# An FFN block product taken out of its accumulation chain and given one full PSUM bank

## The chip, the cores and the metric

The kernel runs on one core of a Trainium2 chip. The time is the device time of one execution in microseconds (us); the median of three runs stands below, and one further execution was profiled. The core's engines run side by side and meet through semaphores: TensorE (PE: matmuls into PSUM; PEld is its weight load), VectorE (DVE), ScalarE (ACT), GpSimd (POOL) and SyncE (SP), which here only issues DMA transfers.

## The reference

Each of the 64 samples of x (64 x 1024) is mixed across its 64 channels with one of 16 condition matrices, then passed through a 1024 x 1024 matrix with a top-1 routed rank-8 correction, and added to x:

```
W = weights[condition];   y = einsum('bct,bcd->bdt', x, W)
logits = y_flat @ gate_w.T + expert_bias;   one_hot = one_hot(argmax(logits))
base   = einsum('bth,oh->bto', y, W_up)
z      = einsum('nh,erh->ner', y_flat, lora_A);   d = einsum('ner,ehr->neh', z, lora_B)
out    = x + base + einsum('neh,ne->nh', d, one_hot)
```

## The kernel before

The 64 samples are taken four at a time, so there are 16 blocks of 256 rows (two tiles t of 128 rows). A block's y and W_up are cut into 2 x 2 parts, and the product is made with seven half-size products (Strassen's scheme with shared sums) in place of eight: `a11`, `a12`, `a22`, `s1`, `s2`, `s4`, `s3`, in the text also p1 (`a11`), p2 (`a12`), p6 (`s2`), p5 (`s1`), p7 (`s3`), p4 (`a22`). Each operand is split into a high and a low part (fp32r), and a product of 512 output columns is 4 (k) x 3 (part pairs) steps; a step is one matmul of 512 columns, or two matmuls into two neighbouring PSUM banks. The two-bank form exists because four of the products also carry 36 router and LoRA columns (292 + 256 columns).

PSUM: `bank_x` and `bank_y` are pairs of banks, `bank_b` and `bank_c` single banks, `y_ps` a pair for the conditioned y. In block q one pair is the "chain" and holds running sums: p1, then p1+p6 (U2), then p1+p6+p7 (U3), then U3+p4 plus the second LoRA correction, which is c21. The other is the "pair": p2 and the first LoRA correction (c11's rest), and a transpose of the second z. Chain and pair change roles from block to block (`chains[par]`, `chains[1 - par]`). c11, c12, c21, c22 are the four quarters of the block's output; DVE adds each PSUM result into the x rows in SBUF (`add_pair` reads 2 x 256 columns of two banks, `add_bank` 512 columns of one), and SP stores them.

The order on every engine is written out by hand in `period(q, par, closing)`; nothing is reordered by a scheduler. Block 0 is written out in the start-up, blocks 1 to 14 run in a loop of two periods a turn, and block 15 is the closing period. In period q, PE makes block q's products, and between them `make_y` for block q+1, four times (t, half): (0,0) after p6, (0,1) after the first LoRA correction, (1,0) after p7, (1,1) after `s4` and its correction. Each `make_y` waits for `y_summed`: the DVE addition `sum_y` that empties `y_ps` of the one before. `make_y` (1,1) so waits for `sum_y(a21, ...)`. The y chain goes on: `make_y` -> ACT `move_small_y` -> DVE `sum_y` -> for the last part POOL `add_s1`, `add_s2` -> ACT `round_s1`, `round_s2` -> DVE `low_operand` -> PE `s1`, `s2`. In DVE's period, `after_p7` and `route(q, 1)` stand directly ahead of `sum_y(a21, ...)`.

Of the kernel before, what the change touches and what calls it, by code (L numbers as in the profile page):

```python
# [5 lines left out]
def adaln_ffn_kernel(  # L6
# [8 lines left out]
    lora_b: bass.AP,  # L15
    out: bass.AP,
):

# [16 lines left out]
    ALU = mybir.AluOpType  # L37
# [7 lines left out]
    P = 128  # L45
# [6 lines left out]
    GC = E + ER  # L52
    BANK = 512
    QUARTER = BANK // 2
    BLOCKS = B // 4
# [13 lines left out]
    with ctx:  # L69
# [6 lines left out]
        def sem(name):  # L76
            return ctx.enter_context(nc.semaphore(name))
# [48 lines left out]
        bank_b = banks("bank_b", 1)  # L126
        bank_c = banks("bank_c", 1)
        y_ps = banks("y_ps", 2)
        chains = [bank_x, bank_y]

        ident_zero = sem("ident_zero")
        ident_done = sem("ident_done")
# [32 lines left out]
        p1_out = sem("p1_out")  # L165
        u2_out = sem("u2_out")
        u3_out = sem("u3_out")
        p5_out = sem("p5_out")
        route_step = sem("route_step")
        z_turned = sem("z_turned")  # L170
# [188 lines left out]
        def _(act):  # L359
# [68 lines left out]
            def move_z(q, par, t, used):  # L428
                act.wait_ge(z_turned, 2 * q + t + 1)
                if used:  # L430
                    act.wait_ge(delta22 if t else delta12, q)
                src = chains[1 - par][:, 1, 0:P] if t else bank_c[:, 0, 0:P]
                act.activation(z_t[t][:, :], src, ACT.Copy).then_inc(z_ready, 1)

            split_x(0, 0, 0, False)
# [84 lines left out]
        def _(pe):  # L520
# [63 lines left out]
            def multiply(op, q, bank, fresh):  # L584
                pe.wait_ge(low[op], q + 1)
                w = w_of[op]
                if op in ROUTED:
                    pieces = [(bank[:, 0, 0:QUARTER + GC], slice(0, QUARTER + GC)),
                              (bank[:, 1, 0:QUARTER], slice(QUARTER + GC, WIDE))]
                elif op == "a22":  # L590
                    pieces = [(bank[:, 0, 0:QUARTER], slice(0, QUARTER)),
                              (bank[:, 1, 0:QUARTER], slice(QUARTER, BANK))]
                else:
                    pieces = [(bank[:, 0, :], slice(0, BANK))]
                for k in range(KH):
                    for a, b in ((0, 0), (0, 1), (1, 0)):
                        for dst, cols in pieces:
                            mm = pe.matmul(dst, hl[op][:, a, k, :], w[:, b, k, cols],  # L598
                                           start=(fresh and k == 0 and a + b == 0),
                                           stop=(k == KH - 1 and a == 1), skip_group_check=not fresh)  # L600
                mm.then_inc(product_done[op], 1)
# [4 lines left out]
            def add_delta_pair(t, bank):  # L606
                for n in range(2):
                    mm = add_delta(t, bank[:, n, 0:QUARTER], lora_b_hl[:, n * QUARTER:(n + 1) * QUARTER])
                return mm
# [9 lines left out]
            def delta12_of(q):  # L619
                add_delta(0, bank_c[:, 0, :], lora_b_hl[:, BANK:O]).then_inc(delta12, 1)  # L620

            def last_product(q, chain):
                pe.wait_ge(u3_out, q + 1)
                multiply("a22", q, chain, False)

            def second_delta(q, chain):
                pe.wait_ge(z_ready, 2 * q + 2)
                add_delta_pair(1, chain).then_inc(delta21, 1)
                pe.wait_ge(p5_out, q + 1)
                add_delta(1, bank_b[:, 0, :], lora_b_hl[:, BANK:O]).then_inc(delta22, 1)  # L630

# [63 lines left out]
            make_y(1, 0, 1, index[0])  # L695
            pe.wait_ge(turned_low, AT["lora", 1] + 1)
            turn_z(bank_c[:, 0, 0:P], 0, 0)
            last_product(0, bank_x)
            delta11_of(0, bank_y)
            make_y(1, 1, 0, index[1])  # L700
            multiply("s4", 0, bank_c, True)
            delta12_of(0)
            turn_second_z(0, bank_y)
            make_y(1, 1, 1, index[1])
            second_delta(0, bank_x)

            def period(q, par, closing):
                chain, pair = chains[par], chains[1 - par]
                pe.wait_ge(c11_out, q)
                multiply("a11", q, chain, True)  # L710
                index = [None, None]
                if not closing:
                    index[0] = load_index(q + 1, 0)
                pe.wait_ge(c21_out, q)
                multiply("a12", q, pair, True)
                pe.wait_ge(p1_out, q + 1)
                multiply("s2", q, chain, False)
                if not closing:
                    make_y(q + 1, 0, 0, index[0])
                pe.wait_ge(c12_out, q)  # L720
                turn_z(bank_c[:, 0, 0:P], q, 0)
                pe.wait_ge(c22_out, q)
                multiply("s1", q, bank_b, True)
                delta11_of(q, pair)
                if not closing:
                    make_y(q + 1, 0, 1, index[0])
                pe.wait_ge(u2_out, q + 1)
                multiply("s3", q, chain, False)
                if not closing:
                    index[1] = load_index(q + 1, 1)  # L730
                    make_y(q + 1, 1, 0, index[1])
                multiply("s4", q, bank_c, True)
                delta12_of(q)
                if not closing:
                    make_y(q + 1, 1, 1, index[1])
                turn_second_z(q, pair)
                last_product(q, chain)
                second_delta(q, chain)

            in_blocks(pe, period)  # L740

# [1 line left out]
        def _(dve):  # L743
# [39 lines left out]
            def score(bank, addend):  # L783
                dve.tensor_tensor(scores[:, :], bank[:, 0, QUARTER:QUARTER + GC], addend[:, :], ALU.add)\
                   .then_inc(route_step, 1)
# [24 lines left out]
            def add_pair(bank, par, t, half):  # L810
                return dve.tensor_tensor(wide(x_part(par, t, half)), bank[:, :, 0:QUARTER], wide(x_part(par, t, half)),  # L811
                                         ALU.add)
# [3 lines left out]

            def after_p1(q, par):
                dve.wait_ge(product_done["a11"], q + 1)
                dve.tensor_tensor(partial[:, :], chains[par][:, 0, QUARTER:QUARTER + GC], bias_sb[:, :], ALU.add)
                add_pair(chains[par], par, 0, 0).then_inc(p1_out, 1)  # L820

            def after_p2(q, par, used=True):
                dve.wait_ge(product_done["a12"], q + 1)
                dve.wait_ge(p1_out, q + 1)
                score(chains[1 - par], partial)
                route(q, 0, used)

            def after_p6(q, par):
                dve.wait_ge(product_done["s2"], q + 1)
                add_pair(chains[par], par, 0, 1).then_inc(u2_out, 1)  # L830

            def after_p5(q, par):
                dve.wait_ge(product_done["s1"], q + 1)
# [2 lines left out]

            def after_delta11(q, par):
                dve.wait_ge(delta11, q + 1)
                add_pair(chains[1 - par], par, 0, 0).then_inc(c11_out, 1)

            def after_p7(q, par):
                dve.wait_ge(product_done["s3"], q + 1)
                score(chains[par], bias_sb)
                add_pair(chains[par], par, 1, 1).then_inc(u3_out, 1)

            def after_delta12(q, par):
                dve.wait_ge(delta12, q + 1)
# [2 lines left out]

            def after_delta21(q, par):
                dve.wait_ge(delta21, q + 1)
                add_pair(chains[par], par, 1, 0).then_inc(c21_out, 1)

            def after_delta22(q, par):
                dve.wait_ge(delta22, q + 1)
# [70 lines left out]
            after_delta12(0, 0)  # L927
            low_operand("a12", a12, 1)
            sum_y(a22, 1, 1, 1)

            def period(q, par, closing):
                after_delta21(q - 1, 1 - par)
                low_operand("s1", s1_sum, q)
                low_operand("s2", s2_sum, q)
                after_delta22(q - 1, 1 - par)
                after_p1(q, par)
                if not closing:
                    for b in range(2):
                        split_x(q + 1, 1 - par, 0, b)
                after_p2(q, par)  # L940
                low_operand("s4", a12, q)
                low_operand("s3", a21, q)
                after_p6(q, par)
                low_operand("a22", a22, q)
                if not closing:
                    split_x(q + 1, 1 - par, 1, 0)
                    sum_y(a11, q + 1, 0, 0)
                    split_x(q + 1, 1 - par, 1, 1)
                    low_operand("a11", a11, q + 1)
                after_p5(q, par)  # L950
                after_delta11(q, par)
                if not closing:
                    sum_y(a12, q + 1, 0, 1)
                    low_operand("a12", a12, q + 1)
                after_p7(q, par)
                route(q, 1)
                if not closing:
                    sum_y(a21, q + 1, 1, 0)
                after_delta12(q, par)
                if not closing:  # L960
                    sum_y(a22, q + 1, 1, 1)

            in_blocks(dve, period)
            after_delta21(BLOCKS - 1, (BLOCKS - 1) % 2)
            after_delta22(BLOCKS - 1, (BLOCKS - 1) % 2)


# [21 lines left out]
```

## Time and profile before

| | |
|---|---|
| median of 3 runs | 445.52 us (444.39 to 446.64) |
| the profiled execution, its own time | 445.25 us |
| its span, first to last instruction | 443.4 us |
| PE busy | 433.8 us, 98% |
| PE weight loads busy | 411.3 us, 93% |
| DVE busy | 351.4 us, 79% |
| ACT busy | 198.3 us, 45% |
| POOL busy | 116.7 us, 26% |
| DMA | 87 GB/s over the span |

Busy shares are averages over the span. PE instructions overlap in the pipeline, so that the duration of a matmul is longer than the distance from its start to the next one's; costs of a group are read as distances between starts. The same holds for DVE, to a lesser degree.

### The profile page before, as it was taken

Reading aid. Unit: us, or ns where it says so; the run is one execution under the profiler, and the core shown is the slowest. Engines: PE = TensorE matmul, PEld = TensorE weight load, DVE = VectorE, ACT = ScalarE, POOL = GpSimd, SP = SyncE. Lnnn points to the kernel's source line nnn. Section 1 sums busy time; section 2 is a strip of 40 time slices with the busy share of each in tenths; the row PEclk is TensorE's granted clock in tenths of the full one; section 3 lists DMA queues with packets and bytes.
Section 4 is the critical chain, followed back from the end, with each engine's and each line's share of the span. In section 5 each row is a group of like instructions: output and inputs, shape, how many; then the busy total and the mean of one; then the engine's idle time right before and its main releaser. Section 6 shows DMA issues by size and latency. Waiting matters only on the chain.

```text
span 443.4 us, 8927 instructions
## 1 busy us (share of the span) xinstructions
PE 433.8 (98%) x3138; PEld 411.3 (93%) x3139; DVE 351.4 (79%) x643; ACT 198.3 (45%) x310; POOL 116.7 (26%) x95
## 2 busy tenths in 40 slices
PE   8899998999999999999999999999999999999996
PEld 8789997999999999999999999999999999999995
DVE  3899879698796969789686969879696978969653
ACT  4895436253544426244543625354352624454210
POOL 3992040130505022050504013050503204050400
PEclk9999999999999999999999999999999999999999
DMA  9900032130412122140313113041212214032102
GB/s 216 406 21 1 2 120 71 54 139 24 148 41 104 61 89 100 47 142 24 118 56 109 71 51 138 24 139 50 98 67 94 95 47 142 24 118 70 50 30 90
DMA packets 17231, 38.73 MB, mean 87 GB/s; under 512 B 3838, under 2 KB 3838, under 8 KB 17218
## 3 DMA queue, kind: packets, MB, share of 16 engines
q1 hardware_dynamic: 16018, 38.02, 24.3%
q10 hardware_dynamic: 1040, 0.26, 0.3%
q0 software_dynamic: 160, 0.28, 0.3%
q8 instruction: 8, 0.13, 0.1%
q14 instruction: 5, 0.04, 0.0%
HBM read 21.78 MB, written 16.78 MB: 87 GB/s over the span
## 4 chain that ended last, share of the span: by engine, by line
PE 82%; DVE 6%; issue 6%; POOL 2%; DMA 2%; ACT 0%; DVEq 0%; POOLq 0%
PE bank_y L598 25%; PE bank_x L598 24%; PE y_ps L534 11%; PE bank_c L598 10%; PE bank_b L598 9%; DMA lora_b_sb<-in_L_ffn_lora_B_dram 2%; DVE w_s L780 1%; DVE w_a L780 1%; DVE x_hl L747 1%; PE bank_y L604 1%; PE bank_c L604 1%; PE bank_x L604 1%; PE bank_b L604 1%; POOL lora_b L305 1%; DVE hl_s L757 1%
## 5 line engine op out<-in xcount | busy, mean ns | idle before, releaser
L310 POOL TENSOR_TENSOR s_sum<-a 128x512 f32<-128x512 f32 x16 | 20.7, 1293 | 294.7 <-DVE a L752 294.7
L368 ACT ACTIVATE x_hl<-x_sb 64x1024 fp32r<-64x1024 f32 x64 | 67.8, 1059 | 58.9 <-DMA x_sb<-in_x_dram 58.1
L747 DVE TENSOR_TENSOR x_hl<-x_sb,x_hl 64x1024 fp32r<-64x1024 f32 x64 | 78.2, 1221 | 9.1 <-ACT x_hl L368 7.2
L598 PE MATMUL bank_x<-w_a,hl_a 128*128 128x292 f32 (+1 forms) x576 | 76.1, 288 | 0.0
L598 PE MATMUL bank_y<-w_a,hl_a 128*128 128x292 f32 (+1 forms) x576 | 76.0, 288 | 0.0
L598 PEld LDWEIGHTS bank_y<-w_a,hl_a 128*128 128x128 f32 x576 | 73.6, 189 | 0.5
L598 PEld LDWEIGHTS bank_x<-w_a,hl_a 128*128 128x128 f32 x576 | 73.5, 189 | 0.5
L372 ACT ACTIVATE y_small<-y_ps 128x512 f32<-128x512 f32 x62 | 37.1, 599 | 74.1 <-PE y_ps L534 74.1
L534 PE MATMUL y_ps<-cond_hl,x_hl 128*128 x496 | 63.8, 272 | 2.5 <-DVE a L752 1.0
L534 PEld LDWEIGHTS y_ps<-cond_hl,x_hl 128*128 128x128 f32 x496 | 61.5, 191 | 5.0 <-DVE a L752 1.4
L752 DVE TENSOR_TENSOR a<-y_ps,y_small 128x512 f32<-128x512 f32 x62 | 42.6, 686 | 13.0 <-ACT y_small L372 12.4
L598 PE MATMUL bank_y<-w_s,hl_s 128*128 128x292 f32 (+1 forms) x384 | 51.5, 290 | 1.2 <-DVE x_sb L811 1.2
L598 PE MATMUL bank_x<-w_s,hl_s 128*128 128x292 f32 (+1 forms) x384 | 51.5, 290 | 0.0
L598 PEld LDWEIGHTS bank_y<-w_s,hl_s 128*128 128x128 f32 x384 | 49.2, 188 | 1.4 <-DVE x_sb L811 1.4
L598 PEld LDWEIGHTS bank_x<-w_s,hl_s 128*128 128x128 f32 x384 | 49.4, 188 | 0.1
L598 PE MATMUL bank_b<-w_s,hl_s 128*128 128x512 f32 x192 | 48.3, 400 | 0.0
L598 PE MATMUL bank_c<-w_s,hl_s 128*128 128x512 f32 x192 | 48.2, 399 | 0.0
L378 ACT ACTIVATE hl_a<-a 128x512 fp32r<-128x512 f32 x48 | 30.1, 627 | 40.2 <-DVE a L752 40.2
L757 DVE TENSOR_TENSOR hl_a<-a,hl_a 128x512 fp32r<-128x512 f32 x48 | 33.6, 700 | 10.6 <-ACT hl_a L378 10.2
L598 PEld LDWEIGHTS bank_c<-w_s,hl_s 128*128 128x128 f32 x192 | 35.0, 189 | 7.3
L598 PEld LDWEIGHTS bank_b<-w_s,hl_s 128*128 128x128 f32 x192 | 35.2, 190 | 6.8
L811 DVE TENSOR_TENSOR x_sb<-bank_y,x_sb 128x512 f32<-128x512 f32 x40 | 27.3, 682 | 16.2 <-PE bank_y L604 16.0
(126 smaller groups left out, 476.5 us busy)
## 6 DMA issues: line engine op xcount, KB each, us to landing
x_sb<-in_x_dram SPq DMA_DIRECT2D x32, 512.0 KB, 3.4
out_dram<-x_sb SPq DMA_DIRECT2D x64, 256.0 KB, 2.0
w_raw<-in_L_ffn_W_up_dram SPq DMA_DIRECT2D x8, 512.0 KB, 11.7
cond_sb<-in_L_cond_weights_dram ACTq DMA_DIRECT2D x1, 256.0 KB, 5.5
cond_sb<-in_L_cond_weights_dram SPq DMA_DIRECT2D x1, 256.0 KB, 6.6
router_sb<-in_L_ffn_lora_A_dram POOLq DMA_DIRECT2D x1, 128.0 KB, 8.1
lora_b_sb<-in_L_ffn_lora_B_dram POOLq DMA_DIRECT2D x1, 128.0 KB, 8.4
router_sb<-in_L_ffn_gate_w_dram POOLq DMA_DIRECT2D x1, 16.0 KB, 6.1
```

Source lines behind the costliest of these rows:

```text
L310: pool.tensor_tensor(s1_sum[:, :], a21[:, :], a22[:, :], ALU.add).then_inc(s1_added, 1)
L368: act.activation(x_hl[rows, t, b, :], x_sb[rows, 2 * par + t, :], ACT.Copy).then_inc(x_high, 1)
L372: act.activation(to[:, :].rearrange("q (g d) -> q g d", d=D), halves_of(bank)[:, :, 1, :], ACT.Copy).then_inc(y_small_out, 1)
L378: act.activation(hl[op][:, 0, :, :], src[:, :].rearrange("q (k n) -> q k n", n=P), ACT.Copy)\
L534: mm = pe.matmul(bank[:, k % KH // 2, at:at + P], x_hl[:, t, b, k * P:(k + 1) * P], cond_hl[:, index[b], :, :], start=True, stop=True)
L598: mm = pe.matmul(dst, hl[op][:, a, k, :], w[:, b, k, cols], start=(fresh and k == 0 and a + b == 0), stop=(k == KH - 1 and a == 1), skip_g ...
L604: return pe.matmul(dst, z_t[t][:, :], src, start=False, stop=True, skip_group_check=True)
L747: dve.tensor_tensor(x_hl[other, t, b, :], x_sb[rows, 2 * par + t, :], x_hl[rows, t, b, :].bitcast(fp32), ALU.subtract).then_inc(x_low, 1)
L752: dve.tensor_tensor(dst[:, :].rearrange("q (g d) -> q g d", d=D), halves_of(bank)[:, :, 0, :], small[:, :].rearrange("q (g d) -> q g d", d ...
L757: dve.tensor_tensor(hl[op][:, 1, :, :], src[:, :].rearrange("q (k n) -> q k n", n=P), hl[op][:, 0, :, :].bitcast(fp32), ALU.subtract).then ...
L780: dve.tensor_tensor(turn_target(op, c, 1), bank.rearrange("q (k n) -> q k n", n=P), turn_target(op, c, 0).bitcast(fp32), ALU.subtract).the ...
L811: return dve.tensor_tensor(wide(x_part(par, t, half)), bank[:, :, 0:QUARTER], wide(x_part(par, t, half)), ALU.add)
```

## The change

From block 1 on the roles are fixed: the chain is always in `bank_y` and the pair always in `bank_x` (block 0 keeps its own). p4 isn't added to the chain any more: it starts fresh in the first bank of the pair, as 12 matmuls of 512 columns, once p2's bank has been read; its LoRA correction is one matmul of 512 columns. DVE adds U3 from the chain into the x rows by an instruction of its own (`add_u3`), behind `route(q, 1)`, and later adds p4 with its correction by `add_bank`. The semaphore `chain_free` tells PE that the chain's banks may be overwritten, and orders the two additions. On DVE, `after_delta21`, the low parts of s1 and s2 and `after_delta22` move from the head of period q+1 to the tail of period q, which in the instruction stream is the same place.

```diff
-        chains = [bank_x, bank_y]
+        def chain_of(q):
+            return bank_x if isinstance(q, int) and q == 0 else bank_y
+
+        def pair_of(q):
+            return bank_y if isinstance(q, int) and q == 0 else bank_x
...
+        chain_free = sem("chain_free")
...
-                elif op == "a22":
+                elif op == "a22" and not fresh:
                     pieces = [(bank[:, 0, 0:QUARTER], slice(0, QUARTER)),
                               (bank[:, 1, 0:QUARTER], slice(QUARTER, BANK))]
...
             def period(q, par, closing):
-                chain, pair = chains[par], chains[1 - par]
+                chain, pair = chain_of(q), pair_of(q)
                 pe.wait_ge(c11_out, q)
+                pe.wait_ge(chain_free, q)
                 multiply("a11", q, chain, True)
...
                 turn_second_z(q, pair)
-                last_product(q, chain)
-                second_delta(q, chain)
+                multiply("a22", q, pair, True)
+                pe.wait_ge(z_ready, 2 * q + 2)
+                add_delta(1, pair[:, 0, :], lora_b_hl[:, 0:BANK]).then_inc(delta21, 1)
+                delta22_of(q)
...
+            def add_u3(q, par):
+                add_pair(chain_of(q), par, 1, 0).then_inc(chain_free, 1)
...
             def after_delta21(q, par):
                 dve.wait_ge(delta21, q + 1)
-                add_pair(chains[par], par, 1, 0).then_inc(c21_out, 1)
+                if isinstance(q, int) and q == 0:
+                    add_pair(bank_x, par, 1, 0).then_inc(c21_out, 1)
+                else:
+                    dve.wait_ge(chain_free, q + 1)
+                    add_bank(bank_x, par, 1, 0).then_inc(c21_out, 1)
...
                 after_p7(q, par)
                 route(q, 1)
+                add_u3(q, par)
                 if not closing:
                     sum_y(a21, q + 1, 1, 0)
```

On DVE, the stretch from the last steps of `route(q, 1)` to the c22 addition, in a loop period that has its chain in `bank_y`. Before, with `a<-y_ps,y_small` being `sum_y`, first a21 and then a22:

```order
131 L792 REGISTER_ALU
132 L807 TENSOR_TENSOR z_parts<-z_sel,z_parts 128x2x32 [waits route_step]
133 L752 TENSOR_TENSOR a<-y_ps,y_small 128x512 [waits y_small_out]
134 L815 TENSOR_TENSOR x_sb<-bank_c,x_sb 128x512 [waits p5_out,delta12]
135 L752 TENSOR_TENSOR a<-y_ps,y_small 128x512 [waits y_small_out]
136 L811 TENSOR_TENSOR x_sb<-bank_y,x_sb 128x512 [waits delta21]
137 L757 TENSOR_TENSOR hl_s<-s_sum,hl_s 128x512 [waits high_s1]
138 L757 TENSOR_TENSOR hl_s<-s_sum,hl_s 128x512 [waits high_s2]
139 L815 TENSOR_TENSOR x_sb<-bank_b,x_sb 128x512 [waits u3_out,delta22]
```

The same stretch in the changed kernel:

```order
130 L799 REGISTER_ALU
131 L814 TENSOR_TENSOR z_parts<-z_sel,z_parts 128x2x32 [waits route_step]
132 L818 TENSOR_TENSOR x_sb<-bank_y,x_sb 128x512
133 L759 TENSOR_TENSOR a<-y_ps,y_small 128x512 [waits y_small_out]
134 L822 TENSOR_TENSOR x_sb<-bank_c,x_sb 128x512 [waits p5_out,delta12]
135 L759 TENSOR_TENSOR a<-y_ps,y_small 128x512 [waits y_small_out]
136 L822 TENSOR_TENSOR x_sb<-bank_x,x_sb 128x512 [waits chain_free,delta21]
137 L764 TENSOR_TENSOR hl_s<-s_sum,hl_s 128x512 [waits high_s1]
138 L764 TENSOR_TENSOR hl_s<-s_sum,hl_s 128x512 [waits high_s2]
```

One instruction, `add_u3` (132), has come between the routing steps and `sum_y` of a21; the c21 addition reads one bank where it read two, and waits for `chain_free` too.

On PE, from p4 to the next block's p1, before:

```order
356 L598 MATMUL bank_y<-w_a,hl_a 128x256 [waits low_a22,u3_out]
357 L598 MATMUL bank_y<-w_a,hl_a 128x256 x23
358 L604 MATMUL bank_y<-lora_b_hl,z_t 128x256 [waits z_ready]
359 L604 MATMUL bank_y<-lora_b_hl,z_t 128x256
360 L604 MATMUL bank_b<-lora_b_hl,z_t 128x512 [waits p5_out]
361 L585 REGISTER_ALU [waits c11_out]
362 L598 MATMUL bank_x<-w_a,hl_a 128x292 [waits low_a11]
```

The same place in the changed kernel:

```order
356 L605 MATMUL bank_x<-w_a,hl_a 128x512 [waits low_a22]
357 L605 MATMUL bank_x<-w_a,hl_a 128x512 x11
358 L611 MATMUL bank_x<-lora_b_hl,z_t 128x512 [waits z_ready]
359 L611 MATMUL bank_b<-lora_b_hl,z_t 128x512 [waits p5_out]
360 L592 REGISTER_ALU [waits chain_free,c11_out]
361 L605 MATMUL bank_y<-w_a,hl_a 128x292 [waits low_a11]
```

24 matmuls of 256 columns have become 12 of 512, two correction matmuls one, the wait for `u3_out` is gone, and p1 of the next block waits for `chain_free` beside `c11_out`.

## Rows read from the trace of the kernel before

**Rows 1.** The page, part 1: busy time (share of the span) and instructions

```profile
PE 433.8 (98%) x3138; PEld 411.3 (93%) x3139; DVE 351.4 (79%) x643; ACT 198.3 (45%) x310; POOL 116.7 (26%) x95
```

**Rows 2.** The page, part 4: chain that ended last, by engine

```profile
PE 82%; DVE 6%; issue 6%; POOL 2%; DMA 2%; ACT 0%; DVEq 0%; POOLq 0%
```

**Rows 3.** Timeline of PE, start us, duration us, second half of period 7

```profile
228.23 0.40 PE L604 MATMUL bank_x<-lora_b_hl,z_t 128*128 128x256 f32 x2
228.47 1.04 PE L534 MATMUL y_ps<-cond_hl,x_hl 128*128 x8
229.34 3.25 PE L598 MATMUL bank_y<-w_s,hl_s 128*128 128x292 f32 x24
...
233.31 3.01 PE L598 MATMUL bank_c<-w_s,hl_s 128*128 128x512 f32 x12
236.16 0.40 PE L604 MATMUL bank_c<-lora_b_hl,z_t 128*128 128x512 f32 x1
236.40 1.00 PE L534 MATMUL y_ps<-cond_hl,x_hl 128*128 x8
237.24 0.30 PE L613 MATMUL bank_x<-ident,z_parts 128*128 128x128 f32 x1
237.29 3.12 PE L598 MATMUL bank_y<-w_a,hl_a 128*128 128x256 f32 x24
240.25 0.40 PE L604 MATMUL bank_y<-lora_b_hl,z_t 128*128 128x256 f32 x2
240.48 0.39 PE L604 MATMUL bank_b<-lora_b_hl,z_t 128*128 128x512 f32 x1
```

**Rows 4.** Timeline of DVE, period 7; in brackets idle before, and releaser

```profile
230.84 0.68 DVE L811 TENSOR_TENSOR x_sb<-bank_x,x_sb 128x512 f32<-128x512 f32 x1
231.43 0.68 DVE L752 TENSOR_TENSOR a<-y_ps,y_small 128x512 f32<-128x512 f32 x1
232.81 0.69 DVE L757 TENSOR_TENSOR hl_a<-a,hl_a 128x512 fp32r<-128x512 f32 x1 [0.70 <-ACT hl_a L378]
...
235.42 0.68 DVE L752 TENSOR_TENSOR a<-y_ps,y_small 128x512 f32<-128x512 f32 x1
...
238.07 0.69 DVE L752 TENSOR_TENSOR a<-y_ps,y_small 128x512 f32<-128x512 f32 x1 [0.78 <-ACT y_small L372]
240.69 0.69 DVE L811 TENSOR_TENSOR x_sb<-bank_y,x_sb 128x512 f32<-128x512 f32 x1 [1.93 <-PE bank_y L604]
...
242.22 1.55 DVE L757 TENSOR_TENSOR hl_s<-s_sum,hl_s 128x512 fp32r<-128x512 f32 x1 [0.15 <-ACT hl_s L378]
```

**Rows 5.** Timeline of PE, `make_y` of periods 1, 6 and 14, part (1,1)

```profile
84.17 1.00 PE L534 MATMUL y_ps<-cond_hl,x_hl 128*128 x8
...
211.05 1.01 PE L534 MATMUL y_ps<-cond_hl,x_hl 128*128 x8
...
413.55 1.00 PE L534 MATMUL y_ps<-cond_hl,x_hl 128*128 x8
```

**Rows 6.** Timeline of DVE, `sum_y` of a21 in periods 1 and 14

```profile
83.19 0.68 DVE L752 TENSOR_TENSOR a<-y_ps,y_small 128x512 f32<-128x512 f32 x1
...
412.54 0.68 DVE L752 TENSOR_TENSOR a<-y_ps,y_small 128x512 f32<-128x512 f32 x1
```

**Rows 7.** Timeline of PE, period 2, where `make_y` (0,1) came late

```profile
101.31 0.39 PE L604 MATMUL bank_y<-lora_b_hl,z_t 128*128 128x256 f32 x2
101.65 1.11 PE L534 MATMUL y_ps<-cond_hl,x_hl 128*128 x8
102.59 0.60 PE L598 MATMUL bank_x<-w_s,hl_s 128*128 128x292 f32 x3
```

**Rows 8.** Timeline of DVE, period 2, `sum_y` of a11 ahead of it

```profile
100.90 0.69 DVE L752 TENSOR_TENSOR a<-y_ps,y_small 128x512 f32<-128x512 f32 x1 [0.27 <-ACT y_small L372]
```

**Rows 9.** Timeline of ACT, period 7: the x rows' split, and `round_s2`

```profile
224.69 2.14 ACT L368 ACTIVATE x_hl<-x_sb 64x1024 fp32r<-64x1024 f32 x2 [3.15 <-DMA x_sb<-in_x_dram]
...
241.55 0.63 ACT L378 ACTIVATE hl_s<-s_sum 128x512 fp32r<-128x512 f32 x1 [0.75 <-POOL s_sum L314]
```

More of the change, by code:

```diff
@@ L431, in move_z @@
                     act.wait_ge(delta22 if t else delta12, q)
-                src = chains[1 - par][:, 1, 0:P] if t else bank_c[:, 0, 0:P]
+                src = pair_of(q)[:, 1, 0:P] if t else bank_c[:, 0, 0:P]
                 act.activation(z_t[t][:, :], src, ACT.Copy).then_inc(z_ready, 1)
@@ L620, in delta12_of, with delta22_of @@
                 add_delta(0, bank_c[:, 0, :], lora_b_hl[:, BANK:O]).then_inc(delta12, 1)
[L622 to L628, printed above, removed]
+            def delta22_of(q):
                 pe.wait_ge(p5_out, q + 1)
@@ L697, in _ @@
             turn_z(bank_c[:, 0, 0:P], 0, 0)
-            last_product(0, bank_x)
+            pe.wait_ge(u3_out, 1)
+            multiply("a22", 0, bank_x, False)
             delta11_of(0, bank_y)
@@ L704, in _ @@
             make_y(1, 1, 1, index[1])
-            second_delta(0, bank_x)
+            pe.wait_ge(z_ready, 2)
+            add_delta_pair(1, bank_x).then_inc(delta21, 1)
+            delta22_of(0)
             def period(q, par, closing):
-                chain, pair = chains[par], chains[1 - par]
+                chain, pair = chain_of(q), pair_of(q)
                 pe.wait_ge(c11_out, q)
+                pe.wait_ge(chain_free, q)
                 multiply("a11", q, chain, True)
@@ L818, in after_p1 @@
                 dve.wait_ge(product_done["a11"], q + 1)
-                dve.tensor_tensor(partial[:, :], chains[par][:, 0, QUARTER:QUARTER + GC], bias_sb[:, :], ALU.add)
-                add_pair(chains[par], par, 0, 0).then_inc(p1_out, 1)
+                part = dve.tensor_tensor(partial[:, :], chain_of(q)[:, 0, QUARTER:QUARTER + GC], bias_sb[:, :], ALU.add)
+                if isinstance(q, int) and q == 0:
+                    part.then_inc(chain_free, 1)
+                add_pair(chain_of(q), par, 0, 0).then_inc(p1_out, 1)
             def after_p2(q, par, used=True):
@@ L824, in after_p2 @@
                 dve.wait_ge(p1_out, q + 1)
-                score(chains[1 - par], partial)
+                score(pair_of(q), partial)
                 route(q, 0, used)
@@ L829, in after_p6 @@
                 dve.wait_ge(product_done["s2"], q + 1)
-                add_pair(chains[par], par, 0, 1).then_inc(u2_out, 1)
+                add_pair(chain_of(q), par, 0, 1).then_inc(u2_out, 1)
             def after_p5(q, par):
@@ L838, in after_delta11 @@
                 dve.wait_ge(delta11, q + 1)
-                add_pair(chains[1 - par], par, 0, 0).then_inc(c11_out, 1)
+                add_pair(pair_of(q), par, 0, 0).then_inc(c11_out, 1)
             def after_p7(q, par):
                 dve.wait_ge(product_done["s3"], q + 1)
-                score(chains[par], bias_sb)
-                add_pair(chains[par], par, 1, 1).then_inc(u3_out, 1)
+                score(chain_of(q), bias_sb)
+                add_pair(chain_of(q), par, 1, 1).then_inc(u3_out, 1)
+            def add_u3(q, par):
+                add_pair(chain_of(q), par, 1, 0).then_inc(chain_free, 1)
             def after_delta12(q, par):
@@ L852, in after_delta21 @@
                 dve.wait_ge(delta21, q + 1)
-                add_pair(chains[par], par, 1, 0).then_inc(c21_out, 1)
+                if isinstance(q, int) and q == 0:
+                    add_pair(bank_x, par, 1, 0).then_inc(c21_out, 1)
+                else:
+                    dve.wait_ge(chain_free, q + 1)
+                    add_bank(bank_x, par, 1, 0).then_inc(c21_out, 1)
             def after_delta22(q, par):
@@ L929, in _ @@
             sum_y(a22, 1, 1, 1)
+            after_delta21(0, 0)
+            low_operand("s1", s1_sum, 1)
+            low_operand("s2", s2_sum, 1)
+            after_delta22(0, 0)
             def period(q, par, closing):
[L932 to L935, printed above, removed]
                 after_p1(q, par)
@@ L961, in period @@
                     sum_y(a22, q + 1, 1, 1)
+                after_delta21(q, par)
+                if not closing:
+                    low_operand("s1", s1_sum, q + 1)
+                    low_operand("s2", s2_sum, q + 1)
+                after_delta22(q, par)
             in_blocks(dve, period)
-            after_delta21(BLOCKS - 1, (BLOCKS - 1) % 2)
-            after_delta22(BLOCKS - 1, (BLOCKS - 1) % 2)
 _INS = ['x', 'itok_B_0_15', 'L0_cond_weights', 'L0_ffn_W_up', 'L0_ffn_gate_w', 'L0_ffn_expert_bias',
```

## The prediction

> **What bounds the kernel now.** I read the page first. PE is busy for 98% of the span and its weight loads for 93% [rows 1], and the chain that ended last lies on PE for 82% [rows 2]; what isn't PE in it lies nearly all in the start-up. So from block 1 on the kernel is a PE stream, and the naive reading is: what shortens a product shortens the kernel, and DVE, at 79%, has room for one more addition. Whether it has that room where the addition is put decides this case, so I went on to the timelines of one loop period, PE and DVE beside each other. The reader is to see three things there.
>
> First, PE's period. `make_y` (1,1) starts at 84.17 in period 1 and at 413.55 in period 14: 13 periods in 329.38 us, 25.34 us each [rows 5].
>
> Second, how tight DVE is behind PE. DVE ends `sum_y` of a21 at 235.42 + 0.68 = 236.10, and PE starts the `make_y` that needs it at 236.40 [rows 3, 4]. In periods 1 and 14 the same distance is 84.17 - 83.87 = 0.30 and 413.55 - 413.22 = 0.33 [rows 5, 6]; over all 14 it is 0.30 to 0.35. DVE's 21% of idle time isn't at this place. It is in front of other instructions: 0.70 us for ACT's rounding of a12, 0.78 for ACT's copy of the small y, 1.93 for the second LoRA correction [rows 4].
>
> Third, what PE pays when `sum_y` is late. Period 2 has such a case at `make_y` (0,1): the addition, itself 0.27 us late through ACT, ended at 100.90 + 0.69 = 101.59 [rows 8], PE began `make_y` 0.06 us later at 101.65, and from the start of the correction ahead to the start of the next product it took 102.59 - 101.31 = 1.28 us [rows 7], where period 7 took 229.34 - 228.23 = 1.11 [rows 3], and the periods with an early addition 1.08. Over the blocks this distance reads 1.00 us plus the time from the correction's start to the addition's end, never under 1.08. For PE a wait costs from the point at which the addition ends 0.08 us behind the correction's start, because the weights of the first matmul have to be loaded behind the wait too.
>
> **The change part by part.**
>
> p4's form. Before, 24 matmuls of 256 columns run from 237.29 to 240.25: 2.96 us. The form that it gets is that of `s4`, 12 of 512 columns from 233.31 to 236.16: 2.85 us [rows 3]. Saving 0.11 us per block. The correction pair takes 240.48 - 240.25 = 0.23, a single one of 512 columns 236.40 - 236.16 = 0.24 [rows 3]: nothing. 15 blocks are changed, so PE's own work shrinks by 15 x 0.11 = 1.6 us. The Trainium skill ("TensorE: Matmul & The Clock Gate", "Back-to-back issue gap") has N/2.4 + 2.5 ns a matmul, by which 12 matmuls fewer give back only 12 x 2.5 = 30 ns a product, 0.45 us in all; the rows say 110 ns, and the sum goes by the rows.
>
> The wait for `u3_out` before p4. U3's addition follows p7 and is over long before 237.29, and PE shows no gap there [rows 3]: removing it gives 0. The new wait for `chain_free` before p1 sits at 240.7; the flag is set by an addition that ends near 236.1 on DVE: 0, with 4.6 us of cover. p2 still waits for c21, as before, and the reads of the fixed pair keep their distances to their writers: 0.
>
> The c21 addition reads 512 columns of one bank in place of 2 x 256; both forms take 0.68 to 0.69 us: 0.
>
> `add_u3`, once per block, is the new work: a 128x512 addition out of PSUM. Back to back such additions start 231.43 - 230.84 = 0.59 us apart, and take 0.68 alone [rows 4]. It stands in front of `sum_y` of a21, and there DVE works without a pause: from 232.81 to 236.10 no row has an idle time before it. So `sum_y` ends 0.60 us later against the DVE work ahead of it (bounds: 0.59 and 0.69, for an instruction behind the short ones of `route`). The Trainium skill ("VectorE: DVE Perf Modes", "The TRN2 errata") gives 120 + FD cycles of 0.96 GHz for VectorE out of PSUM, 658 ns for 512 columns; by it the sum below would be 14 x 0.06 = 0.8 us higher.
>
> What it costs there. Now the addition ends 236.10 - 236.16 = -0.06 us from the correction's start; with `add_u3` it ends at +0.54. The free point is +0.08, so PE stands for 0.46 us at `make_y` (1,1), in each of the periods 1 to 14. The closing period makes no y and doesn't pay.
>
> Can DVE win this back over the period? Only if the chain from one `make_y` (1,1) to the next has a gap that waits for PE. I followed it: `make_y` -> ACT -> `sum_y` of a22 (238.07) -> POOL, two additions -> ACT `round_s2` (241.55) -> DVE's low part of s2 at 242.22, which waited for just that (0.15) and not for PE [rows 4, 9] -> then DVE without a pause, or the store and load of x that hang on its c22 addition and end at ACT's split at 224.69 [rows 9] -> `sum_y` of a11 -> ... -> the 0.70 us round trip to ACT -> `route` -> `sum_y` of a21. No link is PE's. From 211.05 to 236.10 this chain takes 25.05 us [rows 4, 5]; over the 13 periods the same distance has a mean of 25.02. With 0.60 for `add_u3`, 0.06 until PE starts, and 0.10 for the exposed weight load (`make_y` lasts 1.11 where it waited, 1.00 where it didn't [rows 5, 7]) the loop becomes 25.78 us, against 25.34. The two workings agree: +0.44 and +0.46.
>
> Where p4's saving goes: p4 isn't in that loop. PE comes 0.11 us earlier to `make_y` (0,1) of the next period and waits there 0.11 longer, since it is already at the edge (1.11 against 1.08 in period 7 [rows 3]). It is kept only for the last two blocks, where no such wait follows: -0.2 us.
>
> Sum: 14 x 0.46 - 0.2 = +6.2 us, against the profiled execution's 445.25 (span 443.4). The median of the runs shown is 445.52, 0.3 higher, so that I put the forecast at 451.5, +1.3%.
>
> **The rivals.**
>
> A, the addition is hidden after all, and only PE's saving is left: 15 x -0.11 = -1.6 us, 443.8. For it speaks DVE's idle time, 3.4 us in the rows shown [rows 4], over five times what is added. It decides if the slack at `make_y` (1,1) is over 0.60; the rows show 0.14 (0.08 + 0.06), and all the idle time behind the place of `add_u3`, which cannot help. This is the rival on the other side, and it would lie within 0.5%. Chance 8%.
>
> B, a part is hidden: the loop is less rigid than I read it, as where the DMA of x sometimes ends the chain at ACT rather than DVE (0.27 us idle [rows 8]) or POOL and DVE slow each other less once their work has shifted (the low part of s2 takes 1.55 us beside POOL, others 0.69 [rows 4]). If half of the 0.46 is won back: 14 x 0.23 = +3.2, 448.6. Chance 12%.
>
> C, more is lost: the inserted addition costs its full 0.69 and PE's wait exposes more of the pipeline, 0.55 to 0.65 per period: +7.5 to +9, 453 to 454.5. For it speaks that the instructions of `route` ahead are short, so less may overlap. Chance 12%.
>
> D, the single-bank form and the removed wait give more than the rows show, and the kernel gets faster by over 0.5% (2.2 us, 443.3): it needs rival A and 0.15 us per block. Chance 2%.
>
> **How the numbers follow.** The likeliest case holds 66%, and its own range is 450.5 to 452.7. With B and C the range is 448.4 to 453.6; outside are A, D and the ends of C. A measurement of this kernel tells about 0.5%, 2.2 us, from no change: slower by more takes the likeliest case, C and nearly all of B, 0.88; within 0.5% are most of A and the rest of B, 0.10; faster 0.02.
>
> **What the changed kernel's profile would show.** PE's period of about 25.8 us instead of 25.34; an idle time before `make_y` (1,1) with DVE's `sum_y` as releaser, some 0.3 to 0.5 us in each of 14 periods, and a distance from the correction ahead to the product behind of 1.59 us where it was 1.13 (237.29 - 236.16); p4 in 2.85 us; at `make_y` (0,1) waits of 0.1 to 0.3 us in most periods; PE's busy share down by about 2 points, DVE's busy time up by 15 x 0.68 = 10 us. DVE's idle time before the c21 addition should fall only by p4's 0.11, to 1.8 us, since what comes before it hangs on the same `make_y`. Wrong would make it: a `sum_y` of a21 that ends less than 0.3 us later against the correction than before, or a wait for PE inside the chain that I called free of it.

## The result and the profile after

The changed kernel takes 451.25 us (451.04 to 451.68, 5 runs) where the kernel before, run beside it, takes 445.32 us (444.39 to 446.64): a ratio of 1.0139, 95% interval 1.0128 to 1.0151. By the ratio it is slower by 6.2 us; the two medians are 5.9 us apart, which is inside the interval (5.7 to 6.7). The profiled execution took 451.25 us, its span is 449.4 us.

Of the page after, the busy times and the shares of the chain that ended last (before: [rows 1], [rows 2]):

```profile
PE 437.7 (97%) x2943; PEld 400.8 (89%) x2944; DVE 360.5 (80%) x658; ACT 198.2 (44%) x310; POOL 116.1 (26%) x95
...
issue 50%; DVE 18%; PE 14%; POOL 9%; DMA 5%; ACT 4%; DVEq 0%; POOLq 0%; SPq 0%; ACTq 0%
```

195 matmuls fewer, 9.1 us more of DVE, and a chain of the end that was 82% PE is now 14% PE: it goes through DVE, POOL, ACT and the DMA of x. In every second period it also runs over p4 and the c21 addition behind it; that this piece doesn't set the pace is not read from the chain but shown by experiment 2. The busy share of PE hardly moves, 98% to 97%, although PE no longer sets the pace; the chain says it, the share doesn't.

The list of waits of the kernel after (engine, line, releaser: us in total, times, longest):

```profile
DVE x_sb L822 <- PE bank_x L611: 27.9, 15, 2.4
...
PEld y_ps L541 <- DVE a L759: 10.9, 20, 1.2
```

PE's weight loads for `make_y` wait 10.9 us for `sum_y`, in 20 places. The same line of the kernel before has 1.4 us in 2 places:

```profile
PEld y_ps L534 <- DVE a L752: 1.4, 2, 1.2
```

Timeline of PE in the kernel after: the second half of a loop period, to be laid beside [rows 3], and the `make_y` (1,1) of the first and the last period:

```profile
84.16 1.11 PE L541 MATMUL y_ps<-cond_hl,x_hl 128*128 x8 [0.19 <-DVE a L759]
...
230.25 0.40 PE L611 MATMUL bank_x<-lora_b_hl,z_t 128*128 128x256 f32 x2
230.49 1.10 PE L541 MATMUL y_ps<-cond_hl,x_hl 128*128 x8
231.43 3.24 PE L605 MATMUL bank_y<-w_s,hl_s 128*128 128x292 f32 x24
...
238.25 0.39 PE L611 MATMUL bank_c<-lora_b_hl,z_t 128*128 128x512 f32 x1
238.83 1.11 PE L541 MATMUL y_ps<-cond_hl,x_hl 128*128 x8 [0.20 <-DVE a L759]
239.78 0.30 PE L620 MATMUL bank_x<-ident,z_parts 128*128 128x128 f32 x1
239.83 2.99 PE L605 MATMUL bank_x<-w_a,hl_a 128*128 128x512 f32 x12
242.65 0.40 PE L611 MATMUL bank_x<-lora_b_hl,z_t 128*128 128x512 f32 x1
...
419.61 1.11 PE L541 MATMUL y_ps<-cond_hl,x_hl 128*128 x8 [0.20 <-DVE a L759]
```

Timeline of DVE in the kernel after, the same period, to be laid beside [rows 4]:

```profile
234.89 0.69 DVE L764 TENSOR_TENSOR hl_a<-a,hl_a 128x512 fp32r<-128x512 f32 x1 [0.70 <-ACT hl_a L385]
...
237.35 0.23 DVE L814 TENSOR_TENSOR z_parts<-z_sel,z_parts 128x64 f32<-128x64 f32 x1
237.49 0.68 DVE L818 TENSOR_TENSOR x_sb<-bank_y,x_sb 128x512 f32<-128x512 f32 x1
238.09 0.68 DVE L759 TENSOR_TENSOR a<-y_ps,y_small 128x512 f32<-128x512 f32 x1
238.69 0.68 DVE L822 TENSOR_TENSOR x_sb<-bank_c,x_sb 128x512 f32<-128x512 f32 x1
240.61 0.69 DVE L759 TENSOR_TENSOR a<-y_ps,y_small 128x512 f32<-128x512 f32 x1 [1.24 <-ACT y_small L379]
243.09 0.69 DVE L822 TENSOR_TENSOR x_sb<-bank_x,x_sb 128x512 f32<-128x512 f32 x1 [1.79 <-PE bank_x L611]
```

The reader is to see: `add_u3` at 237.49, `sum_y` of a21 behind it, over at 238.77, and `make_y` (1,1) beginning 0.06 us later at 238.83. Its bracket shows only 0.20 us of idle PE, since the pipelined ends of the matmuls ahead cover the rest. Read it as a distance: from the correction at 238.25 to p4 at 239.83 it is 1.58 us, against 1.13 before. All 14 periods show it (1.55 to 1.59), and (419.61 - 84.16) / 13 gives 25.80 us a period, where [rows 5] gave 25.34. Thirteen periods longer by 0.46 make 6.0 us, which is the difference of the two spans, 449.4 - 443.4. The fourteenth stall is the one ahead of 84.16, and it doesn't show there, because this execution came 0.36 us earlier out of its start-up: the first `make_y` (0,1) starts at 54.45, in the profiled execution of the kernel before at 54.81. p4 takes 242.65 - 239.83 = 2.82 us here and 2.85 in the mean of the periods, where it took 2.96, and hardly anything of that is seen in the time.

### The profile page after: what moved, and what is told of

Its sections match the earlier page's. It is cut to its first block, busy times and chain, and to the rows that moved or that the text cites. A ratio compares the mean times of both kernels' runs of the same rounds, so it can differ in the third digit from the quotient of the medians.

```text
span 449.4 us, 8559 instructions
## 1 busy us (share of the span) xinstructions
PE 437.7 (97%) x2943; PEld 400.8 (89%) x2944; DVE 360.5 (80%) x658; ACT 198.2 (44%) x310; POOL 116.1 (26%) x95
## 4 chain that ended last, share of the span: by engine, by line
issue 50%; DVE 18%; PE 14%; POOL 9%; DMA 5%; ACT 4%; DVEq 0%; POOLq 0%; SPq 0%; ACTq 0%
PE bank_x L605 5%; POOL a L324 3%; DMA x_sb<-in_x_dram 3%; POOL s_sum L321 3%; POOL s_sum L317 3%; DVE x_sb L818 3%; DVE x_sb L822 2%; PE bank_x L639 2%; DVE a L759 2%; PE bank_y L605 2%; DVE x_hl L754 2%; DMA out_dram<-x_sb 2%; PE y_ps L541 2%; DVE hl_a L764 2%; DVE hl_s L764 2%
## 5 line engine op out<-in xcount | busy, mean ns | idle before, releaser
L605 PE MATMUL bank_x<-w_a,hl_a 128*128 128x292 f32 (+2 forms) x588 | 99.4, 323 | 0.0
L605 PE MATMUL bank_y<-w_s,hl_s 128*128 128x292 f32 x720 | 96.6, 290 | 1.2 <-DVE x_sb L818 1.2
L605 PEld LDWEIGHTS bank_y<-w_s,hl_s 128*128 128x128 f32 x720 | 92.3, 188 | 1.4 <-DVE x_sb L818 1.4
L605 PEld LDWEIGHTS bank_x<-w_a,hl_a 128*128 128x128 f32 x588 | 85.2, 189 | 6.7
L541 PEld LDWEIGHTS y_ps<-cond_hl,x_hl 128*128 128x128 f32 x496 | 60.4, 191 | 13.0 <-DVE a L759 10.9
L541 PE MATMUL y_ps<-cond_hl,x_hl 128*128 x496 | 66.1, 276 | 4.9 <-DVE a L759 3.4
L605 PEld LDWEIGHTS bank_y<-w_a,hl_a 128*128 128x128 f32 x384 | 50.5, 188 | 1.5
L605 PE MATMUL bank_y<-w_a,hl_a 128*128 128x292 f32 (+1 forms) x384 | 51.1, 288 | 0.0
L818 DVE TENSOR_TENSOR x_sb<-bank_y,x_sb 128x512 f32<-128x512 f32 x61 | 41.5, 680 | 0.2 <-PE bank_y L605 0.2
L764 DVE TENSOR_TENSOR hl_s<-s_sum,hl_s 128x512 fp32r<-128x512 f32 x32 | 37.9, 1185 | 3.8 <-ACT hl_s L385 2.6
L385 ACT ACTIVATE hl_s<-s_sum 128x512 fp32r<-128x512 f32 x32 | 20.1, 633 | 40.8 <-POOL s_sum L317 30.2
```

Of the source, the lines that this page charges most:

```text
L385: act.activation(hl[op][:, 0, :, :], src[:, :].rearrange("q (k n) -> q k n", n=P), ACT.Copy)\
L541: mm = pe.matmul(bank[:, k % KH // 2, at:at + P], x_hl[:, t, b, k * P:(k + 1) * P], cond_hl[:, index[b], :, :], start=True, stop=True)
L605: mm = pe.matmul(dst, hl[op][:, a, k, :], w[:, b, k, cols], start=(fresh and k == 0 and a + b == 0), stop=(k == KH - 1 and a == 1), skip_g ...
L764: dve.tensor_tensor(hl[op][:, 1, :, :], src[:, :].rearrange("q (k n) -> q k n", n=P), hl[op][:, 0, :, :].bitcast(fp32), ALU.subtract).then ...
```

## The experiments

The theory (T1): VectorE's chain from one `make_y` (1,1) to the next was 0.14 us short of PE's period; `add_u3` lengthens it by 0.60 us at the one place where DVE has no idle time, and from then on it sets the period. The rivals: T2, the cost is PE's own, through the fixed banks, `chain_free` or p4's form; T3, DVE is so full that 0.60 us more cost their time wherever they stand. "The kernel before" was run again on each chip; every ratio is to those runs.

**1. The U3 addition late.**

```diff
                 route(q, 1)
-                add_u3(q, par)
                 if not closing:
                     sum_y(a21, q + 1, 1, 0)
                 after_delta12(q, par)
                 if not closing:
                     sum_y(a22, q + 1, 1, 1)
+                add_u3(q, par)
```

> The changed kernel with the U3 addition moved on VectorE from in front of sum_y of a21 to behind sum_y of a22, where VectorE waits 1.8 us for the second LoRA correction. Theory T1 (the loss is VectorE's loop, lengthened by 0.60 us at this one place): the stall at make_y (1,1) is gone, the period falls from 25.8 to about 25.2 us, and p4's 0.11 us is kept in most periods: about 1.5 us under the kernel before, 443.8 (443.0 to 444.6, ratio 0.9965). Rival T2 (the loss comes from the fixed roles of the banks, the chain_free wait or p4's form on TensorE): the time stays near 451. Rival T3 (one more addition costs its time wherever it stands, since VectorE is full): also near 451.

Measured: 444.36 us, ratio 0.9995 (0.9986 to 1.0004). The same instructions in the same banks, one of them elsewhere, and 6 us are gone: T2 and T3 both fall, as far as 6 us go. DVE in this kernel:

```profile
234.82 0.69 DVE L759 TENSOR_TENSOR a<-y_ps,y_small 128x512 f32<-128x512 f32 x1
236.00 0.69 DVE L822 TENSOR_TENSOR x_sb<-bank_c,x_sb 128x512 f32<-128x512 f32 x1 [0.49 <-PE bank_c L611]
237.48 0.69 DVE L759 TENSOR_TENSOR a<-y_ps,y_small 128x512 f32<-128x512 f32 x1 [0.78 <-ACT y_small L379]
238.09 0.68 DVE L818 TENSOR_TENSOR x_sb<-bank_y,x_sb 128x512 f32<-128x512 f32 x1
240.01 0.69 DVE L822 TENSOR_TENSOR x_sb<-bank_x,x_sb 128x512 f32<-128x512 f32 x1 [1.25 <-PE bank_x L611]
```

The wait for the second correction falls from 1.93 [rows 4] to 1.25 us: `add_u3` (238.09), 0.60 us in the stream, lies in it, and p4 ends 0.11 us sooner. But I had expected 1.5 us less than the kernel before, p4's saving, and it isn't there. Experiments 6 to 8 look for it.

**2. p4 in 24 matmuls again**, in the changed kernel, so that only PE's own work grows.

```diff
+                elif op == "a22":
+                    pieces = [(bank[:, 0, 0:QUARTER], slice(0, QUARTER)),
+                              (bank[:, 0, QUARTER:BANK], slice(QUARTER, BANK))]
...
```

What is left out sets the start flag of the accumulation on the first half alone, since both halves now lie in one bank.

> The changed kernel with p4 again as 24 matmuls of 256 columns, into the one bank. T1 (TensorE waits for VectorE in every period, p4 isn't in the loop): the 0.11 us more per block shorten TensorE's wait at make_y (0,1) and cost nothing but some 0.2 us at the end: 451.3 (451.0 to 451.8). T2 (TensorE still sets the period): 15 x 0.11 = 1.6 us more, 452.9.

Measured: 450.82 us, ratio 1.0141 (1.0125 to 1.0156), the changed kernel's own ratio being 1.0139. PE has 1.6 us more to do and the time doesn't move. Timeline of PE in this kernel:

```profile
230.26 0.40 PE L616 MATMUL bank_x<-lora_b_hl,z_t 128*128 128x256 f32 x2
230.49 1.00 PE L541 MATMUL y_ps<-cond_hl,x_hl 128*128 x8
231.33 3.26 PE L608 MATMUL bank_y<-w_s,hl_s 128*128 128x292 f32 x24
...
238.73 1.11 PE L541 MATMUL y_ps<-cond_hl,x_hl 128*128 x8 [0.18 <-DVE a L764]
```

From the correction to the next product at `make_y` (0,1) it is now 231.33 - 230.26 = 1.07 us, PE's least; with the short p4 it was 231.43 - 230.25 = 1.18. One period alone proves little, since this distance changes from period to period. In the mean of the last 13 it is 1.12 here and 1.25 with the short p4 (1.14 in the kernel before). So the 0.11 us that p4 saves stand there as waiting.

The same trace shows that p4 isn't in DVE's loop. With the long p4 the c21 addition starts 4.39 us after `make_y` (1,1), with the short one 4.28 (means of 13 periods); the low part of s2, which comes behind it on DVE, starts at 5.92 and 5.90. In both it starts 0.03 us after the end of ACT's `round_s2`.

**3 and 4. One idle instruction in the kernel before**, a DVE reduction whose result nobody reads, once in front of `sum_y` of a21, once behind `sum_y` of a22.

```diff
+            def extra():
+                dve.tensor_reduce(extra_sb[:, 0:1], w_of["a22"][:, 0, 0, 0:512].bitcast(fp32), AX.X, ALU.max)
...
                 route(q, 1)
+                extra()
```

> The kernel before, nothing else changed, with one VectorE reduction over 512 columns to a scratch column in front of sum_y of a21 in periods 1 to 15; its result is used nowhere. If it takes about 0.6 us in the stream, T1 expects what the change cost, 14 x 0.46 = +6.4 us, about 451.7 (450.5 to 453), with a wait of TensorE at make_y (1,1) behind VectorE. T2: no change, 445.3, since banks, form and waits of TensorE are those of before.

> The kernel before with the same VectorE reduction behind sum_y of a22, ahead of the wait for the second LoRA correction (1.93 us idle). T1: within 0.5 us of the kernel before, 445.3. T3 (added VectorE time costs wherever it stands): as in front of sum_y of a21, about 451.

Measured: in front, 450.54 us, ratio 1.0135 (1.0120 to 1.0151); behind, 444.59 us, ratio 0.9999 (0.9990 to 1.0009). The kernel before, with its banks, its chain and its p4, becomes as slow as the changed one by 0.60 us of DVE at that place, and doesn't notice it behind `sum_y` of a22, 3.3 us later (237.97 - 234.70). DVE with the reduction behind, then in front:

```profile
234.70 0.69 DVE L754 TENSOR_TENSOR a<-y_ps,y_small 128x512 f32<-128x512 f32 x1
...
237.97 0.68 DVE L849 TENSOR_REDUCE extra_sb<-w_a 128x1 f32<-128x512 f32 x1
```

```profile
237.11 0.68 DVE L849 TENSOR_REDUCE extra_sb<-w_a 128x1 f32<-128x512 f32 x1
237.71 0.68 DVE L754 TENSOR_TENSOR a<-y_ps,y_small 128x512 f32<-128x512 f32 x1
```

The price in the stream is 237.71 - 237.11 = 0.60 us, as for `add_u3` (238.09 - 237.49).

**5 and 10. How much is free there.** The same reduction over 64 and over 256 columns.

> The kernel before with a VectorE reduction over 64 columns (in place of 512) in front of sum_y of a21. T1 with the slack read from the trace (0.14 us at make_y (1,1)): if it takes 0.13 to 0.2 us in the stream, 14 x (0 to 0.06) = 0 to 0.8 us more than the kernel before, against 6 us for the 0.60 us of the longer one; a cost in proportion to VectorE's time without slack would be 14 x 0.17 = 2.4 us.

> The kernel before with a VectorE reduction over 256 columns in front of sum_y of a21. Over 64 columns it took 0.13 us in the stream and cost nothing, over 512 columns 0.60 us and cost 6 us. T1, with free slack of 0.14 us and full cost beyond: about 0.33 us in the stream, 14 x 0.19 = +2.7 us, ratio 1.006 (1.0045 to 1.0075). Without a free part, in proportion to 6 us for 0.60: +3.3 us, ratio 1.0075.

Measured: 64 columns, 444.38 us, ratio 0.9999 (0.9990 to 1.0008); 256 columns, 447.58 us, ratio 1.0055 (1.0041 to 1.0069), +2.5 us. DVE over 64 columns, then over 256:

```profile
234.49 0.21 DVE L849 TENSOR_REDUCE extra_sb<-w_a 128x1 f32<-128x64 f32 x1
234.62 0.68 DVE L754 TENSOR_TENSOR a<-y_ps,y_small 128x512 f32<-128x512 f32 x1
```

```profile
236.33 0.41 DVE L849 TENSOR_REDUCE extra_sb<-w_a 128x1 f32<-128x256 f32 x1
236.66 0.68 DVE L754 TENSOR_TENSOR a<-y_ps,y_small 128x512 f32<-128x512 f32 x1
```

0.13 us in the stream cost nothing, 0.33 cost 2.5, 0.60 cost 6.0. Divided by 14 periods, the last two are 0.18 and 0.43: both lie 0.15 to 0.17 us under what was added, the free part that the trace gave as 0.14. A cost in proportion (3.3 us for 0.33) lies outside the interval of +1.8 to +3.1.

**9. Only `sum_y` of a21 moved**, ahead of `route`; `add_u3` stays.

```diff
+                if not closing:
+                    sum_y(a21, q + 1, 1, 0)
                 route(q, 1)
                 add_u3(q, par)
-                if not closing:
-                    sum_y(a21, q + 1, 1, 0)
```

> The changed kernel with nothing moved but sum_y of a21, which now stands ahead of route; the U3 addition stays behind route, where the change put it. T1: the U3 addition no longer lies between p7 and make_y (1,1), so the stall there goes and the time is that of the late addition, 444.3 (443.8 to 444.8), limited by make_y (0,1). If the place of the U3 addition behind route itself were what costs (through c12's addition behind it, or z), the time stays near 451.

Measured: 444.84 us, ratio 0.9994 (0.9985 to 1.0003). `add_u3` behind `route` costs nothing once no one waits behind it.

**6. The late U3 addition with p4 in 24 matmuls**, the edits of 1 and 2 together.

> The changed kernel with the U3 addition late, and p4 as 24 matmuls of 256 columns. The late addition alone was 0.2 us under the kernel before where 1.5 us had been expected, so p4's saving was not seen. T1a (the saving is swallowed by the wait at make_y (0,1), behind sum_y of a11): 24 matmuls cost 0 to 0.5 us, 444.4 to 444.9, ratio to the kernel before 1.000. T1b (the saving was real, and something else in the changed kernel costs 1.3 us): 1.6 us above the late addition alone, 446.0, ratio 1.003.

Measured: 444.28 us, ratio 1.0001 (0.9991 to 1.0010). That is T1a: beside experiment 1 (0.9995) p4's form is worth 0.3 us by the ratios, which the intervals don't tell from nothing, and not the 1.6 us of T1b. With `add_u3` out of the way PE is still held at `make_y` (0,1) by `sum_y` of a11: from the correction to the next product it is 1.16 us with the short p4 and 1.12 with the long one (means of the last 13 periods), PE's least being 1.08. The two traces have 25.28 and 25.32 us a period, so that some 0.04 of the 0.11 us may be kept.

**7 and 8. Each `sum_y` ahead of the work that it stood behind**, in the changed kernel with the late addition, and in the kernel before.

```diff
-                    split_x(q + 1, 1 - par, 1, True)
+                    split_x(q + 1, 1 - par, 1, True, [0])
+                    move_small_y(q + 1, 0, 0)
                 move_z(q, par, 0, True)
                 if not closing:
-                    move_small_y(q + 1, 0, 0)
+                    split_x(q + 1, 1 - par, 1, True, [1])
...
+                    sum_y(a11, q + 1, 0, 0)
                     split_x(q + 1, 1 - par, 1, 0)
-                    sum_y(a11, q + 1, 0, 0)
                     split_x(q + 1, 1 - par, 1, 1)
                     low_operand("a11", a11, q + 1)
                 after_p5(q, par)
+                if not closing:
+                    sum_y(a12, q + 1, 0, 1)
                 after_delta11(q, par)
                 if not closing:
-                    sum_y(a12, q + 1, 0, 1)
                     low_operand("a12", a12, q + 1)
...
```

and `sum_y` of a21 ahead of `route`, as in 9. The first piece is ACT's: it copies the small y for a11 between the two halves of its split of x, so that the earlier `sum_y` of a11 on DVE has its input. All these moves are made together; only that of a21 was also run alone, in experiment 9.

> The changed kernel with the U3 addition late, and each sum_y ahead of the VectorE work that it stood behind: a11 ahead of the split of x (ScalarE copies its small y between the two halves of its split), a12 ahead of the addition of c11, a21 ahead of route. T1: all waits of TensorE for y_summed go, p4's 0.11 us is kept, and the period is TensorE's own, 25.34 - 0.18 of waits - 0.11 = 25.05 us: 14 x 0.29 = 4.1 us under the kernel before, 440.5 (439.5 to 442), ratio 0.991. T2 (TensorE itself sets the period by other means): no gain over the late addition alone, 444.4.

> The kernel before with the same reordering of sum_y, p4 still in the chain in two banks. T1: the period is TensorE's own with the longer p4, 25.34 - 0.18 = 25.16: 2.5 us under the kernel before, 442.1, and 1.6 us above the reordered changed kernel; that difference is what p4's form is worth once TensorE waits for nothing.

Measured: changed kernel reordered, 441.74 us, ratio 0.9940 (0.9927 to 0.9952); kernel before reordered, 442.73 us, ratio 0.9964 (0.9951 to 0.9977). The first is the fastest of all, 0.0060 x 444.4 = 2.7 us under the kernel before. Timeline of PE in it, `make_y` (0,1) with its neighbours, and the first and last `make_y` (1,1):

```profile
83.09 1.00 PE L542 MATMUL y_ps<-cond_hl,x_hl 128*128 x8
...
225.86 0.40 PE L612 MATMUL bank_x<-lora_b_hl,z_t 128*128 128x256 f32 x2
226.10 1.01 PE L542 MATMUL y_ps<-cond_hl,x_hl 128*128 x8
226.94 3.24 PE L606 MATMUL bank_y<-w_s,hl_s 128*128 128x292 f32 x24
...
410.02 1.00 PE L542 MATMUL y_ps<-cond_hl,x_hl 128*128 x8
```

The distance at `make_y` (0,1) is 226.94 - 225.86 = 1.08, the least, and the period (410.02 - 83.09) / 13 = 25.15 us. The same two rows of the reordered kernel before, (410.94 - 82.89) / 13 = 25.24 us a period:

```profile
82.89 1.00 PE L535 MATMUL y_ps<-cond_hl,x_hl 128*128 x8
...
410.94 1.01 PE L535 MATMUL y_ps<-cond_hl,x_hl 128*128 x8
```

Both directions came out as T1 expects, both sizes too large. I had taken 0.18 us a period for PE's waits in the kernel before; the period of the reordered one says 25.34 - 25.24 = 0.10. And p4's form is worth 0.09 us a period and 1.0 us in all (442.73 - 441.74), where I had written 1.6.

## Why the prediction was right

Forecast 451.5 us (448.4 to 453.6), slower with a chance of 0.88; measured 451.25 us, by the ratio +6.2 us beside the forecast +6.2. That the two agree to 0.1 us is partly luck, since the runs of one kernel differ by more: the kernel before took 444.39 to 446.64.

- **The bound before.** PE, with DVE 0.14 us behind it at `make_y` (1,1): shown by experiments 5, 10 and 3. The first puts the free part at 0.13 or more, the other two at 0.15 and 0.17. PE wasn't quite alone: the reordered kernel of experiment 8 has a period shorter by 0.10 us, the waits for `sum_y` that the kernel before had at `make_y` (0,1) and (1,0): the distances there shrink by 0.06 and 0.03 us in the mean.
- **The price of `add_u3`**, 0.60 us in the stream: measured 238.09 - 237.49 = 0.60. The higher figure to which the Trainium skill ("VectorE: DVE Perf Modes", "The TRN2 errata") led, 0.06 more an instruction, isn't what this stream shows; it stands near the duration of one alone, 0.68.
- **The stall**, 0.46 us, with a distance of 1.59 from the correction to the next product: measured 1.58, and 0.06 us from the end of `sum_y` to PE, in all 14 periods.
- **No link of the loop is PE's** but `make_y` itself: 25.78 us forecast, 25.80 measured. The forecast called this a second working that agrees with the stall; it isn't an independent one, since its 25.02 is PE's period of 25.34 less the same distance of 0.30 to 0.35 at `make_y` (1,1). What bears it out is experiment 2, where PE's work is longer without any effect and the low part of s2 keeps its distance to ACT; the idle time ahead of the c21 addition is 1.79 us where I wrote 1.8.
- **p4's saving is swallowed at `make_y` (0,1)**: shown by 2, where the wait shrinks by 0.13 us in the mean as p4 grows. Its size in the rows, 0.11, is nearer to 0.09 a period where PE runs free. The part at the end of the program that should be kept, 0.2 us, is under what the times can tell; in the traces of experiments 7 and 8 it is there, 439.7 - 410.02 against 440.8 - 410.94 us from the last `make_y` (1,1) to the end, 0.2 less.
- **The removed wait for `u3_out`, the new one for `chain_free`, the c21 addition's form**: nothing each. Experiments 1 and 9 bound them together: the changed kernel without the stall is at 0.9995 and 0.9994. Together they are bounded, not each alone.
- **Rival A** (hidden in DVE's idle time) asked the right question, where the idle time lies: the same 0.60 us is free 3.3 us later (experiment 4). **B**, half won back, and **C**, more lost, did not occur.
- **Small things that came out otherwise.** PE's busy share was to fall by about 2 points and fell by 0.4 (433.8 of 443.4, 437.7 of 449.4): a stalled `make_y` counts as busy for longer (66.1 us in all where it was 63.8, by part 5 of the pages). DVE's busy time rose by 9.1 us, not 10. And 6.2 us more than the median of the kernel before, 445.52, would be 451.7; the 451.5 is the sum on the profiled execution's 445.25.

My one clear miss came behind the prediction, in the expectation for experiment 1. I let p4's saving come back as soon as the stall at `make_y` (1,1) was gone, against my own reading that `make_y` (0,1) was already at the edge. With two places on one loop at nearly zero slack, to clear one returned next to nothing of what the other held.

## What to carry to other kernels

An engine that is idle for a fifth of the span can have no room at all where an instruction is put: before adding work to it, find the next instruction on it that the bounding engine waits for, and take the distance from that one's end to the waiting instruction as the budget, less what the waiting engine needs behind a late release. Here that was 0.30 us less 0.16 (0.06 until PE starts, 0.10 for its longer first matmuls); the distance alone would have promised twice the room that there was. Two lines of order decided 6 us here, the same instruction being free on the other side of `sum_y`. And where two engines are within 1% of each other, as here (0.14 us of room in a period of 25.34), clear the waits first and shorten the bounding engine's work afterwards: p4's better form was worth nothing that these runs can tell in the old order, and 1.0 us in the new one.

## What the runs showed of the hardware

A short wait of TensorE costs more than its idle time shows. Where `sum_y` was late, the idle time in the bracket was 0.20 us, while the distance from the correction to the next product grew by 0.45 us: the matmuls ahead still drain in the same stretch, and the eight matmuls behind the wait took 1.11 us to their end where they took 1.00. Their first weight load no longer lies beside other matmuls. PE's weight loads for `make_y` (1,1), in the kernel before and then after:

```profile
236.16 1.09 PEld L534 LDWEIGHTS y_ps<-cond_hl,x_hl 128*128 128x128 f32 x8
```

```profile
238.83 0.97 PEld L541 LDWEIGHTS y_ps<-cond_hl,x_hl 128*128 128x128 f32 x8 [0.62 <-DVE a L759]
```

Before, the first load starts together with the correction (236.16), 0.24 us ahead of the first matmul at 236.40 [rows 3]. After, it starts together with the first matmul, at 238.83: it waits for `sum_y` too.
